# One reduction over both score banks of a fill in place of one reduction for each bank

## The reference: a dense mixture of experts, an attention, and the experts again

```python
x = x + 0.5 * ffn(layernorm(x))       # 32 experts of 96, every token through every expert,
                                      # weighted by a routed softmax (top 8, cut at 0.8)
x = x + attn(layernorm(x))            # 16 heads of 16, 4 key/value heads, rotary, softmax
x = x + 0.5 * ffn(layernorm(x))

# inside attn, for each head and each query
scores = einsum('bhqd,bhkd->bhqk', q, k) * scaling
attn   = softmax(scores, axis=-1)     # needs the maximum over all 1024 keys
out    = einsum('bhqk,bhkd->bhqd', attn, v)
```

## Time and profile before

| | us |
|---|---|
| median of 3 runs | 2366.85 |
| lowest and highest | 2366.6, 2366.93 |
| the profiled execution | 2365.77 |
| its span | 2364.0 |
| PE busy | 2279.1 (96%) |
| DVE busy | 1570.8 (66%) |
| ACT busy | 1236.7 (52%) |
| POOL busy | 1050.9 (44%) |
| DVE line 857, the maxima, 1024 instructions | 657.7 |
| PE line 1100, their scores, 1024 matmuls | 311.9 |

### The profile page before, as it was taken

How to read it: one execution, slowest core, us unless ns; L and a number is a source line. 1 busy time by engine, 2 the same in 40 slices (tenths; PEclk the granted TensorE clock), 3 DMA queues, 4 the chain that set the end, 5 groups by cost and what they waited for, 6 DMA issues and landing times.

```text
span 2364.0 us, 48461 instructions
## 1 busy us (share of the span) xinstructions
PE 2279.1 (96%) x19616; PEld 1517.4 (64%) x19616; DVE 1570.8 (66%) x3107; ACT 1236.7 (52%) x1966; POOL 1050.9 (44%) x863
## 2 busy tenths in 40 slices
PE   0899999999999999999999999999999999999999
PEld 0788875555555556556555555555655665688887
DVE  7656558877777777777777776776776763354543
ACT  3333332466665666666566566656666656633332
POOL 0666663443443443344334343433433434366665
PEclk9999999999999999999999999999999999999999
DMA  5210111011011011001101001010010000011010
GB/s 203 77 36 29 36 48 49 10 26 41 17 31 42 15 34 30 27 22 41 29 19 51 20 22 36 23 33 19 22 30 22 13 30 19 15 33 29 19 38 19
DMA packets 96343, 80.24 MB, mean 34 GB/s; under 512 B 40308, under 2 KB 88692, under 8 KB 95736
## 3 DMA queue, kind: packets, MB, share of 16 engines
q1 hardware_dynamic: 95976, 77.11, 11.4%
q10 hardware_dynamic: 144, 0.03, 0.0%
HBM read 64.25 MB, written 12.85 MB: 33 GB/s over the span
## 4 chain that ended last, share of the span: by engine, by line
PE 92%; DVE 6%; issue 1%; SPq 0%; ACT 0%; DMA 0%; POOL 0%; POOLq 0%; DVEq 0%; ACTq 0%
PE PS L1070 42%; PE PS L1088 21%; PE PS L1100 11%; PE PS L1131 11%; PE PS L1042 2%; DVE arena L857 1%; PE PS L1112 1%; PE PS L1017 1%; PE PS L1045 1%; PE PS L1172 1%; PE PS L1158 1%; DVE arena L834 0%; DVE amax L698 0%; PE PS L1026 0%; DVE WGU L709 0%
## 5 line engine op out<-in xcount | busy, mean ns | idle before, releaser
L1070 PE MATMUL PS<-XT,WGU 128*128 128x256 f16 x9216 | 1117.1, 274 | 48.9 <-DVE WGU L709 32.0
L1070 PEld LDWEIGHTS PS<-XT,WGU 128*128 128x128 f16 x9216 | 875.0, 98 | 279.8 <-issue 131.9
L519 POOL TENSOR_TENSOR arena<-arena 128x512 f16<-128x512 f32 x384 | 447.3, 1165 | 1197.4 <-ACT arena L594 1197.4
L857 DVE TENSOR_REDUCE arena<-PS 128x1 f32<-128x512 f32 x1024 | 657.7, 684 | 369.6 <-PE PS L1100 367.6
L617 ACT ACTIVATE arena<-PS,fac 128x512 f32<-128x512 f32 x1024 | 647.4, 685 | 236.2 <-PE PS L1112 234.9
L587 ACT ACTIVATE arena<-PS,fac 128x512 f32<-128x512 f32 x384 | 264.0, 688 | 760.6 <-PE PS L1070 760.6
L1088 PE MATMUL PS<-WD,arena 128*128 128x256 f16 x4608 | 568.0, 273 | 1.8 <-POOL arena L519 1.6
L1088 PEld LDWEIGHTS PS<-WD,arena 128*128 128x128 f16 x4608 | 432.3, 98 | 141.5 <-issue 89.9
L514 POOL TENSOR_TENSOR arena<-arena 128x512 f32<-128x512 f32 x384 | 492.9, 1284 | 47.0 <-DVE arena L842 45.6
L834 DVE SCALAR_TENSOR_TENSOR arena<-arena,PS 128x512 f32<-128x512 f32 x384 | 261.0, 680 | 281.2 <-ACT arena L587 280.7
L1100 PE MATMUL PS<-arena 48*128 48x512 f16 x1024 | 311.9, 382 | 7.4 <-DMA arena<-k_scratch 4.6
(11 more groups left out here) (115 smaller groups left out, 835.0 us busy)
## 6 DMA issues: line engine op xcount, KB each, us to landing
arena<-ce_scratch SPq DMA_DIRECT2D x256, 128.0 KB, 3.3
arena<-wgu SPq DMA_DIRECT2D x2, 3072.0 KB, 16.1
arena<-q_scratch SPq DMA_DIRECT2D x96, 64.0 KB, 2.2
arena<-ktab_c SPq DMA_DIRECT2D x16, 256.0 KB, 4.1
q_scratch<-arena SPq DMA_DIRECT2D x32, 128.0 KB, 1.7
out<-X SPq DMA_DIRECT2D x8, 512.0 KB, 3.0
X<-wd SPq DMA_DIRECT2D x1, 3072.0 KB, 26.3
X<-x SPq DMA_DIRECT2D x1, 3072.0 KB, 15.4
```

The source lines that it names most:

```text
L519: pool.tensor_tensor(hs[1][:, d % HS, :], tw[d % 2], hs[0][:, d % HS, :], ALU.subtract).then_inc(lo_done, 1)
L857: dve.tensor_reduce(mx[:, half * REP * QT + c:half * REP * QT + c + 1], PS[:, B_MAX + half, :], AX_X, ALU.max).then_inc(max_taken, 1)
L1070: ins = pe.matmul(PS[:, b, j * HALF_G:(j + 1) * HALF_G], WGU[w][:, kt, part * CHUNKS + c + j, :], XT[r][:, k % 2, kt, half * HALF_G:(half ...
```

## The change

The two reductions of a fill become one that reads both banks, 1024 columns, into one place. DVE waits for both halves of the scores before it. It counts `max_taken` up once a fill. PE waits once a fill, before the first half, for the reduction of the whole fill before. `mx` shrinks to half, and the instruction that joined the two halves in `max_rows` is gone.

```diff
-               (QT * P, F32), (QT * P, F16), (QT * P, F16), (2 * REP * QT, F32), (QT * REP, F32),
+               (QT * P, F32), (QT * P, F16), (QT * P, F16), (REP * QT, F32), (QT * REP, F32),
...
-                for half in range(2):
-                    dve.wait_ge(max_ready, 2 * f + half + 1)
-                    dve.tensor_reduce(mx[:, half * REP * QT + c:half * REP * QT + c + 1], PS[:, B_MAX + half, :], AX_X,
-                                      ALU.max).then_inc(max_taken, 1)
+                dve.wait_ge(max_ready, 2 * f + 2)
+                dve.tensor_reduce(mx[:, c:c + 1], PS[:, B_MAX:B_MAX + 2, :].rearrange("p b n -> p (b n)"), AX_X,
+                                  ALU.max).then_inc(max_taken, 1)
...
-                dve.wait_ge(max_taken, 2 * FILLS * (u + 1))
+                dve.wait_ge(max_taken, FILLS * (u + 1))
...
-                link(dve.tensor_tensor(mx[:, 0:REP * QT], mx[:, 0:REP * QT], mx[:, REP * QT:], ALU.max))
-                link(dve.tensor_scalar(ml[:, 0:REP * QT], mx[:, 0:REP * QT], 1 / M_UNIT, None, ALU.mult))
-                link(dve.scalar_tensor_tensor(ml[:, REP * QT:], mx[:, 0:REP * QT], 1 / M_UNIT, ml[:, 0:REP * QT],
+                link(dve.tensor_scalar(ml[:, 0:REP * QT], mx, 1 / M_UNIT, None, ALU.mult))
+                link(dve.scalar_tensor_tensor(ml[:, REP * QT:], mx, 1 / M_UNIT, ml[:, 0:REP * QT],
                                               ALU.mult, ALU.subtract))
...
-                if f:
-                    pe.wait_ge(max_taken, 2 * f - 1 + half)
+                if f and not half:
+                    pe.wait_ge(max_taken, f)
```

## The result

| | median us | range | runs |
|---|---|---|---|
| before | 2366.85 | 2366.38 to 2367.14 | 5 |
| the change | 2377.31 | 2376.38 to 2379.69 | 5 |

The change is slower by 10.5 us: ratio 1.0046, 95% interval 1.0031 to 1.006. The sign is as forecast and the time lies in the range given; the size is twice the 4.9 us of the likeliest case.

The account below looks back on a forecast made before the run. PE, busy for 96% of the span, was taken to bound the kernel, not DVE. Terms 0 + 2.9 + 0.3 + 1.7 = 4.9 us on 2366.85 gave 2371.8 us; range for 8 in 10: 2367.5 to 2381.5.

Parts of the forecast that it names:

- One instruction of 1024 columns: DVE's maxima: one reduction takes about 1217 ns, saving DVE 0.07 us a fill, 36 us in all, none reaching the end.
- (a): 156 fills following at 1.95 us with DVE idle: about 0.02 us of margin left, so no PE stall, 0 us.
- (b): Visits up to 441 us, where PE already stopped between halves: waiting for whole fills loses 2.9 us.
- Type one: Nine early fills where PE's second half started late: eight lose 0.16 us each, 1.3 us.
- Type two: Where DVE is full (373 to 393, 424 to 431 us): delay returns a slot later, 1.3 us over three slots, then 0.1.
- (c): Fills at 1060 and 1888 us, where PE already waited for the second bank: 2 x 0.16 = 0.3 us.
- (d): PE work waiting for the gated product or what DVE queues behind it: delays and real waits lose 1.7 us.
- Rival one: The close fills lack margin, as reading two banks or the semaphore costs more: 2381.5 us; chance 0.22 including a two-pass instruction.
- Rival two: DVE's idle time and existing waits absorb the losses: only +1.5 us, 2368.4; chance 0.17.
- Rival three: DVE sets PE's pace at more places than thought and its relief wins: -5 us, 2361.8; chance 0.05.
- The line on 865: Removing the joining instruction frees 16 x 0.32 us of idle DVE; at most two PE waits shrink by 0.2.
- Signs named ahead: Trace checks: PE idle in 352 to 440 us grows 3 us, last maxima some 4 later, PE busy 539 of 540.

Follow-up runs that it names:

- With the clock at 1.00: The changed kernel plus 12, 12 and 5 extra matmuls into an unused bank before the score matmuls of fills 10, 13 and 16: 2375.99 us.
- the kernel with the two lines as reductions: The changed kernel with DVE lines 778 and 790 written as reductions of the same size, what they compute left out: 2376.48 us.

## Why the prediction was right in sign and too small

- **One instruction of 1024 columns.** Right: 1223 ns against 1217, DVE 34.6 us less busy. That no DVE time reaches the end holds for the kernel before. Under the two waits of the change the shorter instruction does count: with both waits and an instruction of line 865's size kept, two reductions stand at +28.5 and one at +14.9.
- **(a) Close fills, term 0.** Off by 1.8 us. The margin was read from one pair of rows and holds for three quarters of the fills; the other 31 of 131 start their reduction 0.07 us later or get PE 0.09 us later after it, and lose 0.03 to 0.13 us each. The kernel with both waits and two reductions, in which every one of these fills loses, shows that the margin is real.
- **(b) The opening, term 2.9 us.** This is the step that failed. It measured 7.8. The argument, that PE waits for a whole fill and that the loss of one slot comes back in the next while DVE is full, was right; both sizes were not. Type one cost 0.30 us a fill (fills 5, 8, 20, 23, 26, 29, 38), not 0.16: I let the second reduction of the slot start 0.07 earlier, but the first one, which waits for both banks, had already made lines 834 and 842 and with them the second 0.14 later. These seven are 2.1 us where 1.3 were forecast. Type two cost 5.4 us between fills 9 and 18, not 1.3. Fills 32 to 36, with the place at 424 to 431 us, cost 0.06 and the visit at 441 us 0.25, as forecast. Missing in type two were two mechanisms that the kernel before does not show in this stretch. The first stands elsewhere in its trace (lines 751 and 753 at 654 us, line 865 at 1134 us): DVE's small operations, moved by the later queue, met POOL's instructions and took 1 us each in two slots. The second is that the clock fell to half behind PE's longer idle. With the clock at 1.00 the opening loses 5.8 us, which makes the clock 2.0; with the clock at 1.00 and the clash of line 778 gone it loses 4.6, which makes that clash 1.2. The remaining 4.6 hold the waits and the second clash. These are readings of one profiled execution of each kernel; the medians show 0.6 to 1.3 us of the clock and nothing sure of the clash.
- **(c) Two later fills, 0.3 us.** 0.31 and 0.37: 0.7.
- **(d) Events and real waits, 1.7 us.** 0.6 net. The places that follow `max_rows` gained 0.1 to 0.3 each from line 865, more than I had left inside this term. That 0.6 lies under the 1.7 is in part this gain.
- **Rival one** (no margin in (a)) holds a small part, 1.8 of the 9.8 us that it was priced at. Rival two (losses absorbed) is refuted by the kernel with the change only from fill 64: +3.1, with 2.9 in its trace. Rival three (DVE sets the pace and its relief wins): DVE does set the pace in the opening, but there the change makes it later, not earlier.
- **The line on 865** was wrong in kind. "Cover for it is the same idle DVE" asked whether DVE had time, not which operation of POOL the ones behind it would meet.
- **Signs named ahead.** PE's idle from 352 to 440 us grew by 5.8 us where 3 were named, and the last maxima start 11 us later, not 4. PE is busy for 538.8 of 540 us from 1400 on, as named. That the total stayed inside the range is owed to its upper end, which was priced for the loss of (a), not for the opening.

What is not settled: how the last 4.6 us of the opening divide between the waits for banks and the remaining clash, and what makes the clock fall in one execution and not in another. Each experiment that removed one moved the others, and which clash happens differs from kernel to kernel.

## What to carry to other kernels

Merging two instructions on an engine with slack gave nothing here; what counts is when its input may start and when its buffers go back, and both moved the wrong way here. Wherever an engine's queue is shifted by some tenths of a microsecond, look which instructions of the other engine on the same port it will now meet. A wait that is added where the consumer already waits should be priced with the round trip through the full queue, and with the clock that PE may lose while it stands.

## What the runs showed of the hardware

- A DVE operation on 4 to 32 columns with its operands in SBUF (tensor_scalar, tensor_tensor, scalar_tensor_tensor) that started during a POOL instruction took until that instruction's end in 47 of 48 cases in the kernel before and 46 of 47 in the change: 1.15 instead of 0.17, 1.18 instead of 0.19, 1.97 instead of 0.16 us. The exception was one beside PARTITION_ALL_REDUCE. A reduction beside POOL kept its 0.19 us.
- A reduction across two PSUM banks runs at the same rate as one within a bank (1223 ns for 1024 columns, 684 for 512).
- After 1.86 and 2.10 us without a matmul in the changed kernel the granted clock fell from 1.00 to 0.50 and stayed there for some 3 us; after 0.79 us it did not. The length of the idle does not decide it alone: 1.62 and 1.85 us (659 and 1137 us) in the kernel before and 1.77 us (667 us) in the change passed without a fall, 1.77 us at the same place in the kernel with the two lines as reductions was followed by one, and with the change for fills 0 to 63 the clock held after 1.86 us and fell behind 2.10.
- PE started 0.06 us after the recorded end of the reduction that it waited for; in the change and in the kernel with both waits and two reductions there are also 18 and 19 fills with 0.14 to 0.15 us.
